# Feed forward of a decoder layer: activation rows transposed by DMAs that SyncE issues, instead of by TensorE with copies on ScalarE

## The reference

```
def _act_quant(x):        # per row, to whole numbers in -128..127
    scale = 127.0 / jnp.clip(jnp.max(jnp.abs(x), axis=-1, keepdims=True), 1e-05)
    return jnp.clip(jnp.round(x * scale), -128.0, 127.0) / scale
def _bitlinear(x, w):     # the weights are rounded to -1, 0, 1 times a mean
    return jnp.einsum('bsi,oi->bso', _act_quant(x), _weight_quant(w))
gate = jax.nn.silu(_bitlinear(x, w_gate))      # 512 -> 2048
up = _bitlinear(x, w_up)                       # 512 -> 2048
x = _layernorm(x + _bitlinear(gate * up, w_down))   # 2048 -> 512
```

## Time and profile before

| | us |
|---|---|
| median of 3 runs | 1809.9 (1809.62 to 1814.53) |
| the profiled execution's own time | 1810.44 |
| its span | 1808.6 |
| PE busy | 1763.2 (97%) |
| DVE busy | 1421.5 (79%) |
| ACT busy | 1182.6 (65%) |
| POOL busy | 1119.6 (62%) |

### The profile page before, as it was taken

How to read it: one execution, slowest core, us unless ns; L and a number is a source line. 1 busy time by engine, 2 the same in 40 slices (tenths; PEclk the granted TensorE clock), 3 DMA queues, 4 the chain that set the end, 5 groups by cost and what they waited for, 6 DMA issues and landing times.

```text
span 1808.6 us, 38071 instructions
## 1 busy us (share of the span) xinstructions
PE 1763.2 (97%) x14193; PEld 1489.8 (82%) x14213; DVE 1421.5 (79%) x3304; ACT 1182.6 (65%) x2709; POOL 1119.6 (62%) x1250
## 2 busy tenths in 40 slices
PE   8999999999998899999999999999999999989997
PEld 7777777778777899999999999899898899975553
DVE  6777778787888677777778788787777777788997
ACT  6778887757755566666667566666566665665665
POOL 3434455654556586786686655677788777552554
PEclk9999999999998999999999999999999999999999
DMA  5223323111105422432432522314323341551221
GB/s 206 76 66 92 106 78 111 42 35 48 43 25 169 146 89 90 152 101 76 152 113 64 184 87 82 109 50 123 96 77 85 96 117 49 125 112 49 71 71 65
DMA packets 107125, 168.46 MB, mean 93 GB/s; under 512 B 29900, under 2 KB 65104, under 8 KB 106944
## 3 DMA queue, kind: packets, MB, share of 16 engines
q1 hardware_dynamic: 88408, 129.75, 23.2%
q0 software_dynamic: 14656, 28.92, 5.9%
q10 hardware_dynamic: 3880, 7.35, 1.4%
HBM read 109.25 MB, written 50.46 MB: 88 GB/s over the span
## 4 chain that ended last, share of the span: by engine, by line
PE 77%; DVE 9%; POOL 6%; DMA 3%; ACT 3%; issue 2%; ACTq 0%; POOLq 0%; DVEq 0%; SPq 0%
PE att_ps_T L554 7%; PE att_ps_SA L1761 5%; PE att_ps_P L1737 5%; PE att_ps_SB L616 4%; PE att_ps_P L554 4%; PE att_ps_P L1725 4%; PE att_ps_P L1789 4%; PE att_ps_SB L602 4%; PE att_ps_T L1725 3%; PE att_ps_O L1725 3%; PE att_ps_T L1737 3%; PE att_ps_P L1775 2%; PE att_ps_O L1737 2%; PE att_ps_P L1800 2%; PE att_ps_SA L2387 2%; PE att_ps_P L2365 2%
## 5 line engine op out<-in xcount | busy, mean ns | idle before, releaser
L1543 POOL TENSOR_TENSOR ca_pr<-ca_pr,ca_rec 112x750 f32<-112x750 f32 x256 | 366.3, 1451 | 185.8 <-DVE ca_rec L2023 182.9
L425 POOL TENSOR_TENSOR sa_p_lo<-sa_pr,sa_p_hi 112x448 fp32r<-112x448 f32 x128 | 146.7, 1160 | 212.4 <-ACT sa_p_hi L722 211.5
L1908 ACT ACTIVATE ca_big<-att_ps_P 126x384 fp32r<-126x384 f32 (+1 forms) x254 | 105.3, 449 | 66.1 <-PE att_ps_P L1775 64.6
L1902 ACT ACTIVATE ca_pr<-att_ps_SA,ca_nmax 112x750 f32<-112x750 f32 x128 | 113.6, 887 | 22.3 <-DVE ca_nmax L2019 11.6
L891 DVE RECIPROCAL sa_sums<-sa_sums 128x224 f32<-128x224 f32 x64 | 99.1, 1548 | 36.0 <-ACT sa_sums L731 35.8
L2028 DVE TENSOR_TENSOR ca_big<-att_ps_P,ca_big 126x384 fp32r<-126x384 f32 (+1 forms) x254 | 119.7, 498 | 6.2 <-ACT ca_big L1908 5.9
L2019 DVE TENSOR_REDUCE ca_nmax<-att_ps_SA 112x1 f32<-112x752 f32 x128 | 119.1, 931 | 1.3 <-PE att_ps_SA L1761 1.2
L2019 DVE TENSOR_REDUCE ca_nmax<-att_ps_SB 112x1 f32<-112x752 f32 x128 | 119.0, 930 | 0.0
L1737 PE MATMUL att_ps_P<-ca_w_hi,ca_ct 128*126 128x256 f32 x558 | 114.1, 283 | 1.4 <-DVE ca_q_lo L2002 1.4
L1902 ACT ACTIVATE ca_pr<-att_ps_SB,ca_nmax 112x750 f32<-112x750 f32 x128 | 113.1, 884 | 0.1
L1775 PEld LDWEIGHTS att_ps_P<-att_ident,ca_pr 64*126 64x126 f32 (+1 forms) x1524 | 85.7, 138 | 15.2 <-issue 10.7
(11 more groups left out here) (355 smaller groups left out, 6693.0 us busy)
## 6 DMA issues: line engine op xcount, KB each, us to landing
ct_kept<-ca_ct SPq DMA_DIRECT2D x8, 1134.0 KB, 9.5
ca_ct<-ct_kept POOLq DMA_DIRECT2D x8, 1134.0 KB, 8.0
ct_kept<-ca_ct SPq DMA_DIRECT2D x8, 1116.0 KB, 12.6
ca_ct<-ct_kept POOLq DMA_DIRECT2D x8, 1116.0 KB, 10.0
sa_xin<-in_x_dram SPq DMA_DIRECT2D x16, 448.0 KB, 4.0
xt_kept<-ca_xt SPq DMA_DIRECT2D x8, 896.0 KB, 5.3
ca_xt<-xt_kept POOLq DMA_DIRECT2D x8, 896.0 KB, 5.1
ternary<-ca_stage SPq DMA_DIRECT2D x36, 172.0 KB, 1.9
```

The costliest lines, as they stand in the source:

```text
L425: pool.tensor_tensor(p_lo[:, h % NB, :], pr[:, h % NB, :], f32(p_hi[:, h % NB, :]), ALU.subtract).then_inc(p_split, 1)
L1543: pool.tensor_tensor(w, w, rec[:, h % PB, c:c + 1].to_broadcast([R, S]), ALU.mult).then_inc(norm_done, 1)
L1902: act.activation(pr[:, h % PB, c, :].rearrange("r (a s) -> r a s", a=2), two_halves(psum[slot]), ACT.Exp, bias=nmax[:, h % PB, c:c + 1], a ...
```

## The change

`dma_start_transpose` on SyncE makes `xqt` (from tile 2 on) and `hqt` (all tiles but the last, in two halves) directly from `xq` and `hq` in SBUF. TensorE's transposes and ScalarE's copies stay for x of tiles 0 and 1 and for the hidden rows of the last tile. `xqt` exists twice. Gate and up use seven different banks instead of four in turn. For tiles 3 to 13, `xr` and `xq` are made by ScalarE; for tiles 0 to 2 by VectorE. Both halves of `hq` stay on VectorE. VectorE's order in a tile is new, and its wait for GpSimd (`y_done`) stands ahead of the memset and `bn_aggr`, no longer ahead of `bn_stats`. Some counters of finished work become columns indexed by the tile, and a few semaphores that nobody waits for are merged or dropped.

```
 def sync(sp):
+    def turn_x(t):
+        sp.wait_ge(xq_done, t + 1)
+        sp.wait_ge(up_filled, FB * (t - 1))
+        sp.dma_start_transpose(xqt[:, t % 2], xq[:, :]).then_inc(xqt_in[t % 2], 16)
+    def turn_hidden(t, half):
+        sp.wait_ge(hq_done[half], t + 1)
+        if half == 0:
+            sp.wait_ge(y_filled, t + 1)
+        sp.dma_start_transpose(hqt[:, half * FC // 2:(half + 1) * FC // 2, :], hq[:, half_of(half)]).then_inc(hqt_in[half], 16)
     def load_fourth():
+        load_x(3)                      # waits xr_done (before: xq_done)
+        turn_x(2)
+        turn_hidden(0, 0)
+        turn_hidden(0, 1)
     def rest():
+        for t in range(1, T):
+            if t > 1:
+                turn_hidden(t - 1, 0)
+            load_residual(t - 1)       # waits y_summed >= t
+            if t > 1:
+                turn_hidden(t - 1, 1)
+            if 4 <= t + 3 < T:
+                load_x(t + 3)
+            if t + 2 < T:
+                turn_x(t + 2)
 def tensor(pe):
     def gate_up(t, first, blocks):     # n = 2 * f + m, m = 0 gate, 1 up
-                    if not first:
-                        pe.wait_ge(used, FB * t + f - 1)
+                    if not first and n == 7:
+                        pe.wait_ge(h_done, FB * t + 2)
+                    elif not first and n == 3:
+                        pe.wait_ge(h_done, FB * t)
+                    elif not first:
+                        pe.wait_ge(used, FB * (t - 1) + f + 1)
     def rest():
+        for f in range(FB):
+            gate_up(1, False, [f])
+        down(0)
+        for t in range(2, T):
+            gate_up(t, False, range(FB))
+            down(t - 1)                # waits hqt_in[0], hqt_in[1]
+        transpose_last()
+        down(T - 1)
 def scalar(act):
     def rest():
+        for t in range(1, T):
+            scale_hidden(t - 1, 0)
+            scale_hidden(t - 1, 1)
+            silu(t, 0)
+            silu(t, 1)
+            if t + 2 < T:
+                round_x(t + 2)         # Copy, scale, bias=ROUND: xr
+            silu(t, 2)                 # waits h_done of block 0
+            if t + 2 < T:
+                quantise_x(t + 2)      # Copy, bias=-ROUND: xq; waits xqt_in of t + 1
+            silu(t, 3)
 def vector(dve):
+    def scale_of_x(t):                 # links.link waits for its own result
+        links.link(tensor_reduce amax)
+        links.link(tensor_scalar amax)
+        inverse = links.mark(reciprocal xscale)
+        tensor_scalar x_unit
+        links.need(inverse)
+        tensor_scalar xscale .then_inc(x_scaled, 1)
     def first(name):                   # "v1": scale_of_x(3) ahead of hidden(1, 1)
     def rest():
+        for t in range(2, T):
+            sums = sum_rows(t - 2)     # add_residual, bn_stats
+            if t + 2 < T:
+                scale_of_x(t + 2)
+            hidden(t, 0)
+            hidden(t, 1)
+            hidden(t, 2)
+            largest(t, 0)
+            hidden(t, 3)
+            scale_of_hidden(t)         # largest(t, 1), then to hscale
+            guess_root(t - 2, sums)    # y_done, memset, bn_aggr, root
+            quantise_hidden(t, 0)
+            quantise_hidden(t, 1)
```

More of the change, by code:

```diff
@@ L2324, in rest @@
             chain = Chain(pool, rs_own, 3 * 5 + 1)
-            for t in range(0, T - 2):
+            for t in range(T - 2):
                 chain.step(lambda per, k: t * per + k)
@@ L2355, in gate_up @@
             if blocks[0] == 0:
[L2356 removed]
+                if t < BY_TENSOR:
+                    pe.wait_ge(xqt_done, t + 1)
+                else:
+                    pe.wait_ge(xqt_in[t % 2], 16 * (t // 2))
             for f in blocks:
@@ L2447, in copy_h, with silu @@
-        def copy_h(t, blocks):
-            for q in blocks:
-                act.wait_ge(ht_filled, FB * t + q + 1)
+            act.activation(xqt[:, t], xt_ps[:, :].rearrange("p (k n) -> p k n", k=KC), ACT.Copy).then_inc(xqt_done, 1)
+        def silu(t, f, first=False):
+            if f == 0:
+                act.wait_ge(x_scaled, t + 1)
+            act.wait_ge(gate_filled, FB * t + f + 1)
+            if FB * t + f >= 2:
+                act.wait_ge(h_done, FB * t + f - 1)
+            act.activation(sg[:, f % 2, :], gate_up_bank(f, 0, first)[:, :], ACT.Silu, scale=x_unit[:, t, 0:1]).then_inc(sg_done, 1)
@@ new lines, in scale_hidden, with round_x, quantise_x @@
+        def scale_hidden(t, half):
+            if half == 0:
+                act.wait_ge(hscale_done, t + 1)
+            part_h = h[:, half_of(half)]
+            act.activation(part_h, part_h, ACT.Copy, scale=hscale[:, t:t + 1], bias=ROUND).then_inc(h_scaled, 1)
+        def round_x(t):
+            act.wait_ge(x_scaled, t + 1)
+            act.activation(xr[:, :], xin[:, :], ACT.Copy, scale=xscale[:, t:t + 1], bias=ROUND).then_inc(xr_done, 1)
+        def quantise_x(t):
+            act.wait_ge(xr_done, t + 1)
+            act.wait_ge(*before_x(t))
+            act.activation(xq[:, :], xr[:, :], ACT.Copy, bias=-ROUND).then_inc(xq_done, 1)
@@ L2450, in copy_h, with copy_last @@
+        def copy_last():
+            for q in range(FB):
+                act.wait_ge(ht_filled, q + 1)
                 if q == 0:
-                    act.wait_ge(y_filled, t + 1)
+                    act.wait_ge(y_filled, T)
                 act.activation(hqt[:, 4 * q:4 * q + 4, :], ht_ps[q % 2][:, :].rearrange("p (k n) -> p k n", k=4),
                                ACT.Copy).then_inc(hqt_done, 1)
-        def scale_h(t, ahead=False):
-            act.wait_ge(hscale_done, t + 1)
-            for half in range(2):
-                if half and ahead:
-                    silu(t + 1, False, [0])
-                part_h = h[:, half * F // 2:(half + 1) * F // 2]
-                act.activation(part_h, part_h, ACT.Copy, scale=hscale[:, 0:1], bias=ROUND).then_inc(h_scaled, 1)
```

364 lines of the change are left out of this document (145 added, 219 removed).

## The result

The changed kernel takes 1815.1 us (median of 20 runs, 1812.2 to 1818.57) against 1810.52 (20 runs, 1808.62 to 1814.9). The ratio of the means is 1.0021, 95% interval 1.0015 to 1.0028: 3.8 us longer (the medians lie 4.6 apart), and within the 0.3% that was named as no change. The forecast was 1811.8. The profiled execution took 1814.73, its span is 1812.1 (forecast 1810.5).

The account below looks back on a forecast made before the run. VectorE's order, not TensorE, was to bound the tile: first residual 1662.8, ten tiles of 11.51, tile 12 10.1, tile 13 to `hscale` 7.1, end 15.4: span 1810.5, median 1811.8 us, no change. Its own range was 1808 to 1815.2, chance 0.60.

Parts of the forecast that it names:

- What sets the tile: Steady stage: VectorE's new order with its waits for ScalarE takes 11.51 us a tile, against 11.48 before.
- the scale of x: Part of VectorE's order in a tile, from two small operations through `x_unit` to the last: 1.40 us in all.
- the wait of hidden block 2: VectorE in the steady tile: hidden block 2 starts at 4.29, not 4.12, behind ScalarE's third silu; 0.17 us.
- The forecast sign of 0.35 idle ahead of the second half: VectorE in the steady stage: about 0.35 us idle ahead of the second half of `hq`, released by ScalarE.
- TensorE's idle time: Steady stage: TensorE idles about 1.1 us a tile, ahead of the last up block, waiting for hidden block 1.
- The transposes: Transposing DMAs on SyncE: a half issues in 1.0 us, lands after 4.6, all hidden, cost 0.
- Rival B: Transposes land late and push `down`, up blocks and hidden block 2: at 10 us, 2.3 us a tile, 1835; chance 0.13.
- a point of 7.6 us: Second half of `hq`: a landing up to 7.6 us behind its issue is hidden, later ones push `down`.
- the moved wait: VectorE's wait for GpSimd, moved behind `bn_stats`: saves nothing, GpSimd being done 3 us ahead of its new place.
- Rival D: GpSimd's store lands late behind the transposes and sets the tile; at 5.0 us costs 0.9 x 10, 1821; chance 0.06.
- The beginning: Up to the first residual: scale of x for tile 3 and the load behind a store put it at 1662.8; 0 to 3 later.
- The end: Behind the last `hscale`: the code is the same in cost, 1808.6 - 1793.18 = 15.4 us, as before.

Follow-up runs that it names:

- e1: Changed kernel with the scale of x worked out three tiles ahead, behind the root's guess from tile 2 on; 1805.13 us, ratio 0.9978 to the kernel before.
- e2: Changed kernel with five more matmuls, their output overwritten, ahead of each `down` in tiles 1 to 12; 1817.39 us.
- e10: Changed kernel with each transpose of a half of `hq` issued three times from tile 3 on; 1837.48 us.
- e4: Changed kernel with VectorE's wait for GpSimd (`y_done`) put back ahead of `bn_stats`; 1858.07 us.
- e5: Changed kernel with the scale of x for tile 3 moved behind hidden block 2 of tile 1, ScalarE's rounding moving with it; 1814.51 us.
- e6: Changed kernel with tile 0's residual loaded ahead of cross-attention's last store; 1813.11 us.
- e7: Changed kernel with 12 matmuls added on TensorE ahead of the last tile's transposes, into a bank nothing reads; 1809.70 us.
- e3: Changed kernel with each transpose of a half of `hq` issued twice from tile 3 on, the extra first; 1812.96 us.
- e8: Changed kernel with each transpose of a half of `hq` issued four times from tile 3 on; 1867.23 us.

## Why the prediction was right, and where not

**What sets the tile: right.** 11.51 forecast, 11.50 measured. e1 and e2 show both halves of the argument: VectorE's order is the bound, TensorE's saving is not. That it fits to 0.01 is luck: some pieces of the sum were off and cancelled. `x_unit` took 0.21 instead of the earlier trace rows's 0.40, which shortened the scale of x from 1.40 to 1.19. The steps from `hscale` to the residual came to 3.08 (1751.81 to 1754.89) instead of 3.02. And the wait of hidden block 2 cost 0.29, not 0.17 (0.96 instead of 0.67). The prediction took the rows of `x_unit` and of `hq` as they stood, and both durations go with what GpSimd does beside them. In the earlier trace rows, `x_unit` ends at 1759.89, and GpSimd's 128x512 subtraction, from 1758.84 on, ends at 1759.87. In the new order that subtraction falls on the first half of `hq` instead, which the earlier trace rows showed clear of it. The forecast sign of 0.35 idle ahead of the second half failed by that.

**TensorE's idle time: right**, 1.1 forecast, 0.97 on the row and 1.02 in the window, at the block and with the releaser named.

**The transposes: hidden, as forecast; their pieces off.** An issue holds the queue for 1.23 us, not 1.0, and even the 128 KB one of x for 1.19, so it doesn't go by size at this end. The landing is 3.4, not 4.6. Rival B's mechanism exists, and e10 has its first visible case, but the step had it wrong: I put the first issue at a fixed -0.9 of the count and let a late landing push block by block, to a point of 7.6 us. I left out that the issue waits for `down`, so that a late landing delays the next issue as well. The circle of 7.3 us is the right way to ask how much room there is. The Trainium skill, page "VectorE: DVE Perf Modes", section "The three transpose paths", has 1309 ns for a 128x128 block by DMA. By that figure a half, eight blocks, would take an estimated 10.5 us. It landed in 3.4 here and held the queue for 1.23: that the figure is near the cost of one issue is seen, that it is the cost of a block is not borne out.

**GpSimd: right**, no gain from the moved wait against before (nothing waits for `y_out` after, and e4's 4.1 us are a price of the new order alone). Rival D did not occur: the stores land in 2.8 (median; 4.2 at most).

**The beginning: right**, F5 at 1655.92 for 1656.0, the residual at 1662.83 for 1662.8, and its releaser the DMA behind the store. How near they are is partly luck, because Y0 came 0.30 later: counted from Y0, F5 was forecast at 15.0 and came at 14.61 (the scale of x in front of it is the one that was 0.2 too long), the residual at 21.8 and came at 21.52. e5 and e6 show the two causes one by one, each worth 1.2 to 1.3 us. From Y0 to the last `hscale` the change costs 1.92 us, the forecast 1.9: the residual came 0.27 earlier than forecast, and the stretch from it to the last `hscale` took 132.57 instead of 132.3.

**The end: wrong.** The step that failed is the sentence "Behind that the code is the same in cost, 1808.6 - 1793.18 = 15.4". The code is the same and the time is not: 16.70, 1.3 us more. TensorE stands idle for 2.37 us ahead of the last transposes, where it was 1.42 before. Of the 0.95 between them, 0.52 is that `down` of tile 12 ends earlier against VectorE, since TensorE is no longer the bound, and 0.51 that the first half of `hq` is longer beside GpSimd (it also starts 0.07 earlier behind `hscale`). The granted clock then falls to 0.50 and the last `down` takes 5.00. e7 shows that this idle time is the cause of the slow `down`. e3 and e2 say so from the other side: there the same gap was 0.66 and 0.71, `down` took 3.62 and the end 15.37 and 15.34. That GpSimd's operation is what stretches `hq` was not tested by an edit; in the changed kernel the first half lasts 1.12 to 1.20 us from tile 2 on, where that operation runs beside it, and 0.69 in tiles 0 and 1, where it doesn't, and in e1 it is stretched only in the last three tiles, where the two meet again. This is a rival that the prediction lacked, a bound that moves off TensorE and thereby slows the matmuls left on the path.

**The size.** The step at the end is 1.28 us where nothing was forecast. 1.92 + 1.28 = 3.2 us of the 3.8 are accounted for. The rest, 0.6 us, may be the longer low clock in tile 2, which costs 0.85 in e7 and nothing in the changed kernel's profile. How often it comes was not counted, so this stays open.

## What to carry to other kernels

Taking work from the engine that bounds the kernel pays only down to the next order of work: add up that order from start to start, its waits included, before counting the saving. Where two engines hand work back and forth, put what needs neither result into the wait. And when a bound leaves TensorE, look at each gap that it gets and at what runs behind it, at the end above all: matmuls there can become slower than before. And a new order changes which instructions of two engines meet: a duration that was read beside one neighbour may not hold beside another.

## What the runs showed of the hardware that I had not expected

- The granted clock fell from full to half, 2.4 to 1.2 GHz, behind gaps of 1.92 us (e1) and 2.37 us (after the change) ahead of the last transposes and of 3.63 to 4.99 us in tile 2, and not behind gaps of 1.42, 0.66 and, in one profile, 3.44 us. The length of the gap alone doesn't tell: in e10 the half of `down` behind 2.44 us took 3.47, and behind 2.43 us (1807.48) it took 1.90. The 16 matmuls behind the last transposes then took 5.00 to 5.30 us instead of 3.62.
- A transposing DMA between two places in SBUF holds SyncE's queue for about the same time for 128 KB (1.19 us) and for 256 KB (1.23 us), and lands after 3.3 and 3.4 us. Plain loads of 256 KB hold it for 0.32 to 0.72 us, and the residual's land after 2.6 before the change and 3.2 after it (medians).
- With several transposes in a row, the last of them, which counts, lands in 2.9 to 3.1 us (medians of e3, e8 and e10), the extra ones ahead of it in 3.3 to 3.7, and two extra issues take up to 3.29 us instead of 2.58.
- VectorE's rounding of 128x512 from float32 to bf16 in SBUF (`hq`) took 0.69 us alone and, in the changed kernel, 1.12 to 1.20 where a GpSimd subtraction of 128x512 was under way when it started.
